# The experts' up-projection with W1 as the stationary operand

## The reference, cut to what matters

```
xn  = layernorm(x)
xe  = xn * ln_g[e] + ln_b[e]                  # per expert
h   = gelu(xe @ W1[e] + b1[e])                # W1[e]: 256 x 1024
y   = h @ W2[e] + b2[e]                       # W2[e]: 1024 x 256
out = sum over the 2 chosen experts of weight * y
```

## Time and profile before

| | |
|---|---|
| median of 3 executions | 2456.93 us (2450.55 to 2460.57) |
| profiled execution, own time | 2452.51 us |
| its span, first to last instruction | 2450.7 us |
| PE busy in the span | 2197.2 us (90%) |
| DVE, POOL, ACT busy | 1595.4, 1358.8, 1166.2 us |
| experts' stage in the span | about 1573 to 2441 us |

### The profile page before, as it was taken

The page is one execution under the profiler, slowest core; times in us unless marked ns, Lnnn a source line. Parts: engine busy times, 40 slices in busy tenths (PEclk is TensorE's granted clock), DMA queues, the critical chain, the costliest instruction groups (busy, mean ns, idle before and its releaser), DMA issues. The chain is left out here.

```text
span 2450.7 us, 38965 instructions
## 1 busy us (share of the span) xinstructions
PE 2197.2 (90%) x10372; PEld 1497.0 (61%) x10373; DVE 1595.4 (65%) x3839; ACT 1166.2 (48%) x2772; POOL 1358.8 (55%) x1442
## 2 busy tenths in 40 slices
PE   6589999999999999999998343699999999999997
PEld 4456666666666666666665342566766766676675
DVE  5478888888888888888887797633333333333332
ACT  3357777777777777777776121022212222212221
POOL 2267777777777777777774000044444444444444
PEclk9789999999999999999998555899999999999999
DMA  7545555555555545555552645712221222122121
GB/s 219 171 135 150 150 156 157 158 157 146 153 156 157 155 143 157 155 157 145 153 157 72 227 151 74 230 31 31 33 34 30 34 34 32 32 34 32 32 34 28
DMA packets 154089, 275.35 MB, mean 112 GB/s; under 512 B 37224, under 2 KB 103401, under 8 KB 153706
## 3 DMA queue, kind: packets, MB, share of 16 engines
q0 software_dynamic: 67088, 150.41, 25.5%
q1 hardware_dynamic: 76298, 107.96, 14.3%
q10 hardware_dynamic: 10576, 15.52, 1.8%
HBM read 236.95 MB, written 36.83 MB: 112 GB/s over the span
## 5 line engine op out<-in xcount | busy, mean ns | idle before, releaser
L521 POOL DMA_INDIRECT arena<-h_tab,src x880 | 937.0, 1065 | 337.3 <-issue 250.7
L663 PE MATMUL psum<-arena 128*128 128x256 f32 x1760 | 488.7, 401 | 51.1 <-DVE arena L756 48.9
L684 PE MATMUL psum<-arena 128*128 128x264 f32 x1760 | 477.8, 395 | 8.9 <-DVE arena L774 8.6
L663 PEld LDWEIGHTS psum<-arena 128*128 128x128 f32 x1760 | 302.4, 191 | 226.6 <-issue 83.9
L1346 ACT ACTIVATE arena<-psum 128x512 f32<-128x512 f32 x212 | 115.0, 594 | 673.0 <-PE psum L1324 673.0
L1307 PE MATMUL psum<-arena 128*128 x856 | 386.7, 594 | 2.3 <-DVE arena L1360 2.3
L1336 PE MATMUL psum<-arena 128*128 x1696 | 383.6, 379 | 0.0
L684 PEld LDWEIGHTS psum<-arena 128*128 128x128 f32 x1760 | 323.9, 191 | 88.9 <-issue 36.7
L1336 PEld LDWEIGHTS psum<-arena 128*128 128x128 f32 x1696 | 314.0, 190 | 38.3
L756 DVE SCALAR_TENSOR_TENSOR arena<-arena,a_dst,psum 128x512 f32<-128x512 f32 x440 | 323.7, 736 | 8.9 <-PE psum L663 7.1
L1354 DVE TENSOR_TENSOR arena<-psum,arena 128x512 f32<-128x512 f32 x214 | 137.8, 686 | 285.0 <-PE psum L1307 285.0
(11 more groups left out here) (201 smaller groups left out, 2205.4 us busy)
## 6 DMA issues: line engine op xcount, KB each, us to landing
arena<-rel_list SPq DMA_DIRECT2D x110, 512.0 KB, 4.5
arena<-h_tab,src POOLq DMA_INDIRECT x880
arena<-in_x SPq DMA_DIRECT2D x14, 896.0 KB, 8.7
arena<-in_W ACTq DMA_DIRECT2D x8, 1024.0 KB, 14.6
arena<-in_W SPq DMA_DIRECT2D x8, 1024.0 KB, 12.9
arena<-ea_slots SPq DMA_DIRECT2D x440, 8.0 KB
h_tab<-arena SPq DMA_DIRECT2D x7, 924.0 KB, 4.5
out_rows<-arena SPq DMA_DIRECT2D x7, 896.0 KB, 4.1
```

The lines of the kernel that those rows point to most:

```text
L521: pool.indirect_dma_start(rows[:, s % RING, k, :], None, d.h_tab[:, :], bass.IndirectOffsetOnAxis(ap=c.src[:, s * U + k:s * U + k + 1], ax ...
L663: last = nc.tensor.matmul(ps[:, HDT + x, y * UE:(y + 1) * UE], hj[:, (s // 2 * 2 + y) % HJ, x * P:(x + 1) * P], oht[:, half % OT, (u + y) ...
L684: last = nc.tensor.matmul(ps[:, AGG, 0:HS], oh[:, a % OH, k, :], rows[:, a % RING, k, :], start=(k == 0), stop=(k == U - 1))
```

## The change

`up` swaps its operands. For each of 8 blocks of 128 hidden units and 2 halves of the features, a 128x128 block of W1 is stationary and the 128 turned tokens are moving (128 columns). The result has hidden units on partitions, as `down` wants it. So the eight transposes and the bias add on DVE are gone. gelu reads the result from PSUM with b1 as a per-partition bias, which needs one ACT instruction per block of 128 hidden units (8 instead of 2). The stationary operand is read from a fixed place: DVE copies the expert's 2x1024 columns of W1 and 8 columns of b1 into one of two buffers for each tile (`weights`), two tiles ahead. b1 is loaded as 64 rows of 128 (32 KB instead of 4 MB) and turned once by PE. The PSUM banks and `hT` are doubled. In `prepare` and `edges`, several semaphores are merged into shared ones with matching counts; the instructions and what they wait for stay the same (two examples are shown).

```diff
@@ prepare (one of several merged semaphores)
-            sp.wait_ge(links_made, 1)
-            sp.wait_ge(cut_made, 1)
+            sp.wait_ge(links_made, 3)
@@ edges (likewise)
-                last.then_inc(summed, 1)
-                dve.wait_ge(summed, ch + 1)
+                last.then_inc(alpha_made, 1)
+                dve.wait_ge(alpha_made, 2 * ch + 1)
@@ route, SP
-            sp.dma_start(c.arena[:, B1_AT:B1_AT + B1_WORDS], d.b1.rearrange("e n -> (e n)").partition_broadcast(P)).then_inc(c.b1_loaded, 16)
+            sp.dma_start(c.b1_rows, d.b1.rearrange("e (h n) -> (e h) n", n=P)).then_inc(c.b1_loaded, 16)
@@ experts, PE
-            def up(e, b):
-                for n in range(HID // 512):
-                    for m in range(KH):
-                        last = nc.tensor.matmul(ps[:, UP + n, :], xT[:, b, m * P:(m + 1) * P], w1[:, ds(e * HID + (m * X * HID + n * 512), 512)],
-                                                start=(m == 0), stop=(m == KH - 1))
-                last.then_inc(up_done, 1)
+            def up(b):
+                for h in range(HC):
+                    for m in range(KH):
+                        last = nc.tensor.matmul(ps[:, UP + 2 * b + h // 4, h % 4 * P:(h % 4 + 1) * P], w_now[:, b, m, h * P:(h + 1) * P],
+                                                xT[:, b, m * P:(m + 1) * P], start=(m == 0), stop=(m == KH - 1))
+                    if h % 4 == 3:
+                        last.then_inc(up_done, 1)
+            pe.wait_ge(c.b1_loaded, 16)
+            nc.tensor.transpose(ps[:, DOWN, 0:X * HC], c.b1_rows, c.ident[0:X * HC, 0:X * HC]).then_inc(b1_turned, 1)
...
-                    e_now, e_next = experts_of(nc, c.tile_e[0:1, ds(i * 2 + b, 2)], mybir.EngineType.PE)
-                    pe.wait_ge(pre_made, i * 2 + (b + 1))
-                    for h in range(HC):
-                        last = nc.tensor.transpose(ps[:, PRET + h // 4, h % 4 * P:(h % 4 + 1) * P], pre[:, h * P:(h + 1) * P], c.ident[:, :])
-                        if h % 4 == 3:
-                            last.then_inc(preT_made, 1)
-
+                    e_now = experts_of(nc, c.tile_e[0:1, ds(i * 2 + b, 1)], mybir.EngineType.PE)[0]
                     pe.wait_ge(xT_copied, i * 2 + (b + 2))
-                    up(e_next, 1 - b)
+                    pe.wait_ge(w_copied, i * 2 + (b + 2))
+                    if b:
+                        pe.wait_ge(gelu_done, i * 4 + 2)
+                    elif not isinstance(i, int):
+                        pe.wait_ge(gelu_done, i * 4)
+                    up(1 - b)
@@ experts, ACT
-                    for n in range(2):
-                        act.wait_ge(preT_made, i * 4 + (2 * b + n + 1))
-                        nc.scalar.activation(hT[:, n * 512:(n + 1) * 512], ps[:, PRET + n, :], ACT.Gelu).then_inc(gelu_done, 1)
+                for n in range(2):
+                    act.wait_ge(up_done, i * 4 + (2 * b + n + 1))
+                    if n == 0 and b:
+                        act.wait_ge(down_done, i * 2)
+                    elif n == 0 and not isinstance(i, int):
+                        act.wait_ge(down_done, i * 2 - 1)
+                    for h in range(4 * n, 4 * n + 4):
+                        last = nc.scalar.activation(hT[:, b, h * P:(h + 1) * P], ps[:, UP + 2 * b + n, h % 4 * P:(h % 4 + 1) * P], ACT.Gelu,
+                                                    bias=b1_now[:, b, h:h + 1])
+                    last.then_inc(gelu_done, 1)
@@ experts, DVE
-            def bias(n, e):
-                for q in range(2):
-                    part = slice(q * 512, (q + 1) * 512)
-                    last = nc.vector.tensor_tensor(pre[:, part], ps[:, UP + q, :], b1[:, ds(e * HID + q * 512, 512)], ALU.add)
-                last.then_inc(pre_made, 1)
+            def weights(b, e):
+                nc.vector.tensor_copy(b1_now[:, b, :], b1[:, ds(e * HC, HC)])
+                for m in range(KH):
+                    last = nc.vector.tensor_copy(w_now[:, b, m, :], w1[:, m, ds(e * HID, HID)])
+                last.then_inc(w_copied, 1)
...
             for b in range(2):
+                e = dve.value_load(c.tile_e[0:1, b:b + 1], min_val=0, max_val=X - 1)
+                weights(b, e)
                 dve.wait_ge(xT_made, b + 1)
-                scale(b, dve.value_load(c.tile_e[0:1, b:b + 1], min_val=0, max_val=X - 1))
+                scale(b, e)
...
-                    dve.wait_ge(up_done, i * 2 + (b + 2))
-                    bias(0, e_next)
+                    dve.wait_ge(gelu_done, i * 4 + (2 * b + 2))
+                    weights(b, e_after)
                     dve.wait_ge(xT_made, i * 2 + (b + 3))
                     scale(b, e_after)
```

More of the change, by code:

```diff
@@ L460, in edges @@
             nc, ctx, "g_hj", "g_relu", "g_square", "g_oh", "g_redtaken", "g_leaky", "g_factor", "g_exp", "g_ex", "g_first")
[L461 to L464, removed]
+        (oht_made, prod_made, msg_made, acc_made, alpha_made, scanned, ends_made, chain_scanned, fall_made,
+         joined, shifted, diag_made, scale_made, rescaled, cleared) = semaphores(
+            nc, ctx, "g_oht", "g_prod", "g_msg", "g_acc", "g_alpha", "g_scanned", "g_ends", "g_cscanned", "g_fall",
+            "g_joined", "g_shifted", "g_diag", "g_scale", "g_rescaled", "g_cleared")
         gathered = semaphores(nc, ctx, *[f"g_gat{k}" for k in range(GATS)])
@@ L808, in chain_tiles @@
                 dve.wait_ge(chained, ch + 1)
-                nc.vector.tensor_tensor_scan(c_fwd[:, b, :], chain_link[:, b, 0:2 * CT], ps[0:H, SM, 0:2 * CT], before, ALU.min, ALU.max).then_inc(chain_fwd, 1)
-                dve.wait_ge(chain_fwd, ch + 1)
+                nc.vector.tensor_tensor_scan(c_fwd[:, b, :], chain_link[:, b, 0:2 * CT], ps[0:H, SM, 0:2 * CT], before, ALU.min, ALU.max).then_inc(chain_scanned, 1)
+                dve.wait_ge(chain_scanned, 2 * ch + 1)
                 nc.vector.tensor_tensor_scan(c_top[:, ::-1], chain_link[:, b, 1:2 * CT + 1][:, ::-1], c_fwd[:, b, ::-1], -BIG, ALU.min, ALU.max
-                                             ).then_inc(chain_top, 1)
-                dve.wait_ge(chain_top, ch + 1)
+                                             ).then_inc(chain_scanned, 1)
+                dve.wait_ge(chain_scanned, 2 * ch + 2)
                 if ch:
@@ L1219, in experts, with take @@
     with ExitStack() as ctx:
-        (x_loaded0, x_loaded1, b2_loaded, xT_made, xT_copied, up_done, pre_made, preT_made, gelu_done, down_done, sum_made, y_made, gate_done, idx_copied) = semaphores(
-            nc, ctx, "e_x0", "e_x1", "e_b2", "e_xT", "e_xTc", "e_up", "e_pre", "e_preT", "e_gelu", "e_down", "e_sum", "e_y", "e_gate", "e_idx")
+        (x_loaded0, x_loaded1, b2_loaded, xT_made, xT_copied, w_copied, b1_turned, b1_made, up_done, gelu_done, down_done, sum_made, y_made, gate_done, idx_copied) = semaphores(
+            nc, ctx, "e_x0", "e_x1", "e_b2", "e_xT", "e_xTc", "e_w", "e_b1t", "e_b1", "e_up", "e_gelu", "e_down", "e_sum", "e_y", "e_gate", "e_idx")
         gate_loaded, y_stored = semaphores(nc, ctx, "e_gat0", "e_gat1"), semaphores(nc, ctx, "e_yst0", "e_yst1")
         x_loaded = (x_loaded0, x_loaded1)
-        w1 = c.arena[:, W1_AT:W1_AT + W1_WORDS]
+        w1 = c.arena[:, W1_AT:W1_AT + W1_WORDS].rearrange("p (k n) -> p k n", k=KH)
         w2 = c.arena[:, W2_AT:W2_AT + W2_WORDS]
-        b1 = c.arena[:, B1_AT:B1_AT + B1_WORDS]
         HC = HID // P
-        at = EX_AT
-        def take(n):
+        at = ACC_AT
+        def take(n, rows=slice(0, P)):
             nonlocal at
@@ L1233, in take @@
             assert at <= LOGITS_AT
-            return c.arena[:, at - n:at]
-        pre = take(HID)
-        hT = take(HID)
+            return c.arena[rows, at - n:at]
+        w_now = take(2 * KH * HID).rearrange("p (b k n) -> p b k n", b=2, k=KH)
+        hT = take(2 * HID).rearrange("p (b n) -> p b n", b=2)
         b2 = take(X * IN)
+        b1 = take(X * HC)
+        b1_now = take(2 * HC).rearrange("p (b h) -> p b h", b=2)
         xt = take(2 * IN).rearrange("p (b i) -> p b i", b=2)
@@ L1243, in experts @@
         ps = c.psum
[L1244 to L1245 removed]
+        UP, DOWN, XT = 0, 4, 6
+        STEPS = MOE_TILES // 2
         lists = c.lists.rearrange("p u n -> p (u n)")
@@ L1288, in _ @@
             turn(0, 1)
-            with pool.Fori(1, PAIRS) as i:
+            with pool.Fori(1, STEPS) as i:
                 for b in range(2):
@@ L1335, in _ @@
                     for h in range(HC):
-                        last = nc.tensor.matmul(ps[:, DOWN + b, 0:IN], hT[:, h * P:(h + 1) * P], w2[:, ds(e_now * IN + h * X * IN, IN)],
+                        last = nc.tensor.matmul(ps[:, DOWN + b, 0:IN], hT[:, b, h * P:(h + 1) * P], w2[:, ds(e_now * IN + h * X * IN, IN)],
                                                 start=(h == 0), stop=(h == HC - 1))
@@ L1341, in _, with gelu @@
         def _(act):
-            with act.Fori(0, PAIRS) as i:
+            act.wait_ge(b1_made, 1)
+            def gelu(i, b):
```

(25 more changed lines are left out.)

70 lines of the change are left out of this document (36 added, 34 removed).

## The result

The changed kernel takes 2419.61 us (median of 4, 2415.01 to 2423.47) against 2457.60 us before (median of 4). The ratio is 0.985, with a 95% interval of 0.982 to 0.988. So it is faster by 38 us, inside the range given, but under half of the 90 us that were forecast (2457 to 2367). The direction was right, the size was not.

What follows compares the result with a forecast made beforehand. PE was taken to bound the experts' stage. 2452.5 us (profiled execution) - 84 (PE steps) - 3 (start) = 2365.5; against the median 2370, so 2367 us was given, 73% likely, with a range of 2356 to 2422 us.

Steps and rivals of the forecast that it cites:

- So PE sets the time there and no wait does.: Experts' stage before the change: PE busy 100 of 100 us, its own instructions making up the 7.99 us step.
- PE per step, -0.79 us.: Experts' loop: transposes save 0.87 us, `up` grows 0.08; new step 7.20 us, -84 us over 106 steps.
- Rivals 1 and 3: Experts' `up`: loads not hidden, pitch 0.190, 2640 us (7%); pitch about 0.122 or equally costly feeding, 2407 us (10%).
- POOL's work per step is unchanged, 4.9 us ... within 7.2.: Experts' loop: POOL's work, from the gate to L1270's end, stays 4.9 us and fits the 7.2 us step.
- the four rivals: Experts' stage: unhidden loads 7%, DVE copies and POOL DMAs excluding each other 7%, pitch or feeding 10%, no change 3%.
- DVE, "hidden both ways": Experts' loop: DVE's two copies at 0.69 us each, or even 1.37, stay hidden within the 7.2 us step.
- Rival 2: Experts' loop: DVE's copies and POOL's indirect DMAs exclude each other, DVE sets a 7.7 us step, 2418 us; 7%.
- show 0.08 us of it at most: Copies on DVE beside POOL's DMAs: the trace rows show at most 0.08 us of the skill's port locking.
- ACT, 2.1 to 2.8 us, hidden.: Experts' loop: eight 128-column gelus take 2.1 to 2.8 us per step on ACT, hidden within 7.2 us.
- The start, -3 us.: Start of the experts' stage: PE's idle time before the first `bias` and first `up` shrinks, -3 us.

Runs made afterwards that it cites:

- e2: Kernel before the change, with POOL's gather of the gates issued ahead of its gather of token rows: 2456.19 us, ratio 0.9995 to the kernel before.
- e1: Changed kernel with POOL's gather of the gates issued ahead of its gather of token rows: 2365.38 us, ratio 0.963 to the kernel before.
- e3: Changed kernel without DVE's copies of W1 inside the loop: 2405.79 us, ratio 0.979 to the kernel before.
- e4: Kernel before the change, with one more gather of the gates on POOL per step, into a spare column: 2537.66 us, ratio 1.034.
- e8: Changed kernel with each copy of W1 made twice, on another chip: 2617.49 us, ratio 0.990 to the kernel before there (2646.55 us).

## Why the prediction was wrong, point by point

- *"So PE sets the time there and no wait does."* Right for before, and e2 confirms it. But the sentence was carried over to the kernel after, and that was the error.
- *PE per step, -0.79 us.* Right. e1 has `up` at 3.57 us (3.52 forecast) and a step of 7.24 (7.20). Its 2365.38 us stand beside the 2367 that were forecast for the change itself. Rivals 1 and 3, on loads and pitch, did not happen: 0.112 us a pair, where the estimate from the Trainium skill's ratio ("TensorE: Matmul & The Clock Gate", section "Back-to-back issue gap") was 0.159. The trace disagrees with that ratio for float32 pairs.
- *"POOL's work per step is unchanged, 4.9 us ... within 7.2."* **This is the step that failed.** The 4.9 us were POOL's own time from gate to the end of L1270's issue. Left out were the landing of the gates (2.3 us from issue, against the 0.95 us that I counted for it) and the DVE work that waits for it before POOL can begin again. From the earlier trace rows and the same trace's landings it could have been added up: L1384 starts at 1798.50, L1270 at 1803.53, plus 2.3 to land, makes 7.3 us, plus 0.2 from the landing to the next add (as from 1813.60 to 1813.82 in the chain above), makes 7.5. The runs show 7.53 on average. None of the four rivals was such a loop. A step of 7.20 was not to be had without shortening this loop. Of the 0.49 us missed per step, 0.29 are the loop as it was (7.53 - 7.24), 0.16 the copies' effect on it, and 0.04 PE's.
- *"Where a stall goes, say what is late next."* The list of waits had it: DVE's b2 add waited for the gates in 6 steps of the kernel before, 14.8 us. I passed over that as too small, but a wait that shows at all has no slack in those steps. The catching up at 7.52 us, shown above, would have given the pace as well.
- *DVE, "hidden both ways".* The copies took 0.71 us each (0.69 forecast). Hidden they were on DVE, but not on POOL. Rival 2 had the exclusion right, and the wrong victim and size. It was not DVE that lost up to 3.6 us; L1280 and L1258 became 0.09 and 0.08 us longer, together the 0.16 us of the loop. That `` "show 0.08 us of it at most" was a wrong reading: the gather at 1159.36 in the same stage lost 0.46 us. The 0.08 fitted here by luck, since L1258 meets the copy with as much left as that row's gather, and I had no loop to add it to.
- *ACT, 2.1 to 2.8 us, hidden.* Eight gelus occupy 8 x 285 ns = 2.3 us a step (233.6 us for 820). Right. The table load in every other step, which I had kept, is gone; it was no cost either way.
- *The start, -3 us.* The first b2 add came 6.5 us earlier. 2.4 of these are a stage that began earlier (the b2 load issued at 1571.13 after 1573.52); the same start was at 1568.58 in e1 and 1578.56 in e3, so that part is not put down to the change. The other 4.1 us answer to the 3 forecast.
- *The sign and the chances.* The forecast gave 90% to faster, and it was faster. That the range held the time is luck: it was drawn up to rivals 2 and 3, and neither is what set the time.

What stays open: the rows show which DVE instructions POOL's DMAs wait for and how long, but not that a port is what they wait for; nor do they tell where within L1280 it loses its usual 0.09 us. In three steps of every kernel here, before and e1 too (two in e4), POOL's scatter-add (L1280) started 1.0 to 1.3 us later than usual, which lengthened the step by about as much where the loop set it; its cause wasn't sought.

## What to carry to other kernels

When one engine sets a loop's time and work is taken from it, the gain ends at the next closed loop. Add that loop up over all engines and DMAs, with landing times and not issue times, before the gain is counted. An engine that is idle half of the time (POOL here) may still lie on such a loop, and then each of its instructions costs its full length. Within a queue, issue first what is awaited first: here the order of two gathers was worth some 53 us of 91.

## What the runs showed of the hardware

- Float32 128x128 loads, 0.19 us each by their records, run beside 128-column matmuls in a row of 32: 0.112 us a pair at the 2.4 GHz level, against 0.110 for transposes with the same columns.
- A gather of one word per partition occupies POOL for 0.95 us and lands 2.3 us after issue; the second is what the consumer sees.
- A POOL indirect DMA that starts while DVE is in an instruction on SBUF operands alone (seen for L763, L748 and L1372) is longer by what DVE has left, less 0.12 to 0.13 us: 0.08 us with 0.21 left, 0.46 with 0.58, 0.51 with 0.64. The Trainium skill ("SBUF — State Buffer", section on who interferes with whom) has the loser blocked for the whole instruction of the other. These rows agree where DVE came first. Where POOL came first they don't show it: L763 took 0.67 to 0.69 us each of 440 times, with gathers of 0.94 us beside it. What a copy usually lost at most was in e8, 0.86 us for 0.68 where it began late in L1259 and ran into L1271.
